# A gated cross-attention layer with a routed feed-forward: the shared first half's down products made as rounded products chunk by chunk, the scatters counted in two semaphores, and three orders changed

## The reference, cut to what matters

```python
x = x + tanh(g_xattn[0]) * xattn(layernorm(x), ctx, ctx, ...)
xf = layernorm(x)
logits = xf @ Wg                       # 16 experts, the two best are kept
gates = softmax(where(mask, logits, -inf))
for e in range(16):
    h = silu(xf @ W1[e] + b1[e]) * (xf @ W11[e] + b11[e])
    y = y + (h @ W2[e] + b2[e]) * gates[:, e, None]
z = silu(xf @ Ws1 + bs1) * (xf @ Ws11 + bs11) @ Ws2 + bs2   # the shared network
x = x + tanh(g_ffn[0]) * (y + z)
```

## Time and profile before

| | |
|---|---|
| median of 3 runs | 568.99 us |
| the profiled execution | 574.73 us |
| its span (first to last instruction) | 572.6 us |
| PE busy | 546.3 us (95%) |
| DVE busy | 353.6 us (62%) |
| POOL busy | 333.2 us (58%) |
| ACT busy | 238.5 us (42%) |

### The profile page before, as it was taken

One profiled execution on the slowest core, in us unless ns is written; L12 is line 12 of the kernel. 1 busy time (PEld: TensorE's weight loads), 2 busy tenths in 40 slices (PEclk: granted clock), 3 DMA queues, 4 the chain that ended last, 5 costly groups with the idle time before them and its releaser, 6 DMA issues.

```text
span 572.6 us, 12049 instructions
## 1 busy us (share of the span) xinstructions
PE 546.3 (95%) x3290; PEld 440.9 (77%) x3291; DVE 353.6 (62%) x861; ACT 238.5 (42%) x788; POOL 333.2 (58%) x273
## 2 busy tenths in 40 slices
PE   7889999999979999988999999999999999999996
PEld 6556667666758878777888888888888888888785
DVE  5757788787678732345665566555665556435677
ACT  1899999999994201202222122221222212232232
POOL 4689999998863486623364674444444830236550
PEclk8999999999999999999999999999999999999999
DMA  8571001000112144335458777656665210113332
GB/s 284 245 300 64 21 20 38 29 26 20 65 39 103 46 166 174 105 98 185 140 177 293 249 287 259 201 201 211 211 211 201 82 46 29 35 54 107 109 111 73
DMA packets 32899, 76.08 MB, mean 133 GB/s; under 512 B 4961, under 2 KB 21857, under 8 KB 29921
## 3 DMA queue, kind: packets, MB, share of 16 engines
q1 hardware_dynamic: 14960, 52.44, 25.5%
q10 hardware_dynamic: 14832, 14.82, 8.0%
q0 software_dynamic: 3072, 8.39, 4.7%
HBM read 54.93 MB, written 18.61 MB: 128 GB/s over the span
## 4 chain that ended last, share of the span: by engine, by line
PE 80%; DVE 8%; issue 5%; another core or an unknown queue 3%; ACT 2%; POOL 2%; DVEq 0%; ACTq 0%; POOLq 0%
PE mid L749 14%; PE big L730 8%; PE big L731 8%; PE big L732 7%; PE big L517 5%; PE big L653 4%; PE mid L740 4%; PE big L651 3%; PE big L652 3%; PE mid L530 3%; PE work L549 3%; PE last L670 2%; PE work L670 2%; PE last L542 2%
## 5 line engine op out<-in xcount | busy, mean ns | idle before, releaser
L939 ACT ACTIVATE last<-arena 128x512 f32<-128x512 f32 x47 | 28.3, 602 | 183.3 <-DVE arena L1409 183.3
L837 ACT ACTIVATE arena<-big,nmax 128x128 f32<-128x128 f32 x256 | 90.7, 404 | 9.0 <-DVE nmax L1061 8.4
L749 PE MATMUL mid<-dring,arena 128*128 x376 | 88.9, 379 | 0.0
L1409 DVE TENSOR_TENSOR arena<-big,bring 128x512 f32<-128x512 f32 x47 | 32.5, 692 | 87.2 <-PE big L732 87.2
L730 PE MATMUL big<-u_hi,xsT_hi 128*128 x188 | 81.8, 435 | 1.6 <-issue 1.6
L1572 POOL TENSOR_TENSOR u_lo<-arena,u_hi 128x2048 fp32r<-128x2048 f32 x16 | 74.4, 4652 | 1.3
L749 PEld LDWEIGHTS mid<-dring,arena 128*128 128x128 f32 x376 | 67.8, 190 | 7.4
L732 PE MATMUL big<-u_hi,xsT_lo 128*128 x188 | 73.5, 391 | 0.0
L731 PE MATMUL big<-u_lo,xsT_hi 128*128 x188 | 73.4, 390 | 0.0
L1548 POOL TENSOR_TENSOR arena<-arena,rinv 128x1024 f32<-128x1024 f32 (+1 forms) x32 | 58.7, 1834 | 13.3 <-DVE rinv L1069 13.0
L1672 POOL TENSOR_TENSOR pool_mark<-mhalf 128x1 f32<-128x1 f32 x15 | 2.9, 194 | 104.0 <-PE big L732 87.6
(11 more groups left out here) (198 smaller groups left out, 1202.9 us busy)
## 6 DMA issues: line engine op xcount, KB each, us to landing
arena<-up_w_dram SPq DMA_DIRECT2D x16, 1024.0 KB, 7.6
bring<-expert_bias_dram SPq DMA_DIRECT2D x16, 640.0 KB
dring<-down_w_dram SPq DMA_DIRECT2D x18, 512.0 KB
sorted_y<-arena ACTq DMA_DIRECT2D x47, 128.0 KB, 1.7
arena<-sorted_x ACTq DMA_DIRECT2D x43, 128.0 KB, 2.1
sorted_x<-dring SPq DMA_DIRECT2D x3, 1536.0 KB, 9.4
arena<-ctx_t_dram ACTq DMA_DIRECT2D x8, 256.0 KB, 2.8
dring<-up_w_dram SPq DMA_DIRECT2D x2, 1024.0 KB, 4.8
```

Source lines behind the costliest of these rows:

```text
L749: i = mm(mid[:, 1, 0:D], gT[:, p, c, :], dring[:, slot, c * D:(c + 1) * D], start=(c == 0), stop=(c == HC - 1))
L837: i = nc.scalar.activation(probs[:, u % 2, h, :], big[:, u % 2, h // 4, (h % 4) * CTX:(h % 4 + 1) * CTX], ACT.Exp, bias=nmax[:, u % 2, h:h ...
L1409: v.tensor_tensor(hb1[:, p, :], big[:, p, 0, :], bring[:, slot, 0:HID], ALU.add).then_inc(h1_ready, 1)
```

## The change

The first half's down products take the form that the second half's had: `shared_down` and `last_down` become one function of a chunk. The hidden chunk goes into the `gg` buffer, its two parts into `first_gs`, the two parts of the down weight into `first_d` (both laid over the part of the arena that held `gshT`). ACT makes the rounded parts, DVE the rests; the rounding of the last pair's transposed rows goes from POOL to ACT and DVE. The first two blocks' transposes go into `big`, and the remaining pieces of the shared half stand ahead of the first block's up product.

```diff
-WARM = 10
+WARM = 20
...
+        first_d = sb("first_d", [P, 2, DCOLS], F32R)
+        first_gs = sb("first_gs", [P, 2, 2, 512], F32R)
...
+        first_bank = (work, last, mid[:, 0, :], mid[:, 1, :])
+        def hidden_chunk(n):
+            return gg[:, n % 2, :] if n < HC * TILES // GROUP else gshT[:, n // HC % 2, n % HC, :]
...
 # PE, attention
-                    elif ahead:
+                    elif ahead and (behind or u == 2):
                         scores(j + 1, u - 2)
-                    if behind and u == 1:
-                        pe.wait_ge(kT_ready, DC * j + 2 * DC) if ahead else pe.wait_ge(o_taken, 2 * j - 1)
+                    if behind and ahead and u == 1:
+                        pe.wait_ge(kT_ready, DC * j + 2 * DC)
                         project_out(j - 1, 1)
...
                     transpose_probs(j, u)
+                    if not behind and u == 2:
+                        scores(j + 1, 1)
+                    if not ahead and u == 0:
+                        pe.wait_ge(o_taken, 2 * j - 1)
+                        project_out(j - 1, 1)
...
 # PE, the shared down product, now of a chunk
+            def shared_down(n):
+                h, c = divmod(n, HC)
+                pe.wait_ge(gs_lo_ready, n + 1)
+                if n == 0:
+                    pe.wait_ge(d_split, 1)
+                    pe.wait_ge(lg_taken, PAIRS)
+                    pe.wait_ge(rank_taken, 1)
...
+                for t in range(GROUP):
+                    if c == 0 and h > 0:
+                        pe.wait_ge(z_taken, GROUP * (h - 1) + t + 1)
...
+                    mm(banks[t][:, 0:D], g_hi, w_hi, start=(c == 0), stop=False)
+                    mm(banks[t][:, 0:D], g_hi, w_lo, start=False, stop=False)
+                    i = mm(banks[t][:, 0:D], g_lo, w_hi, start=False, stop=(c == HC - 1))
...
             shared_up(0, 3)
+            shared_down(0)
             pe.wait_ge(xfT_kept, 4)
...
+            for n in range(4, 8):
+                shared_up(1, n - 4)
+                shared_down(n - 3)
+            shared_down(5)
             pe.wait_ge(xfT_kept, PAIRS)
...
+            for n in range(8, 15):
+                shared_up(n // HC, n % HC)
+                shared_down(n - 2)
...
+            shared_up(3, 3)
+            shared_down(13)
+            shared_down(14)
+            transpose_rows(0, 0, big[:, 0, 0, :])
+            transpose_rows(1, 1, big[:, 0, 1, :])
+            shared_down(15)
+            pe.wait_ge(xsT_ready, 2)
+            pe.wait_ge(gsh_ready, HC * TILES // GROUP)
             up(0, 0)
-            pe.wait_ge(xsT_ready, 2)
-            shared_down(3, range(1, GROUP))
-            pe.wait_ge(z_taken, 4 * GROUP)
+            pe.wait_ge(z_taken, TILES)
...
 # PE, the end
-            for n in range(2, 4 * HC):
+            for n in range(2, 4 * HC - 2):
                 shared_up(4 + n // HC, n % HC)
-                last_down(n - 2)
-            last_down(4 * HC - 2)
-            last_down(4 * HC - 1)
+                shared_down(TILES + n - 2)
+            shared_up(7, HC - 2)
+            shared_up(7, HC - 1)
+            shared_down(TILES + 4 * HC - 4)
+            for n in range(4 * HC - 3, 4 * HC):
+                shared_down(TILES + n)
...
 # ACT
+            shared_silu(0, 0)
+            act.wait_ge(w_even, 32)
+            nc.scalar.activation(first_d[:, 0, :], dring[:, 0, :], ACT.Copy).then_inc(d_hi_done, 1)
+            round_hidden(0)
+            act.wait_ge(xfT_ready, PAIRS)
+            nc.scalar.activation(xfT_hi[:, :, 2 * P * LAST:2 * P * PAIRS], xfT[:, :, :], ACT.Copy).then_inc(xfT_hi_kept, 1)
...
+            for n in range(8, 16):
+                shared_silu(n // HC, n % HC)
+                round_hidden(n)
...
 # DVE, ahead of the places
+            keep_rest(0)
+            dve.wait_ge(d_hi_done, 1)
+            v.tensor_tensor(first_d[:, 1, :], dring[:, 0, :], first_d[:, 0, :], ALU.subtract).then_inc(d_split, 1)
             shared_hidden(0, [2])
...
+            for n in range(8, 15):
+                shared_hidden(n // HC, [n % HC])
+                if n % HC == 1:
+                    add_shared(n // HC - 1)
+                keep_rest(n)
...
 # DVE, the end: the last chunk's gated product ahead of keep_rest(14), the last two combines behind keep_rest(15)
...
 # POOL, opening: bo_g behind the first normalise, the key weight's split in two pieces at units 0 and 1
+            normalise(0, 0)
             pool.wait_ge(bo_loaded, 16)
             pool.wait_ge(tanh_ready, 1)
             g.tensor_tensor(bo_g, bo_bc, tanh_g[:, 0:1].to_broadcast([P, D]), ALU.mult).then_inc(bo_ready, 1)
-            normalise(0, 0)
-            pool.wait_ge(bo_ready, 1)
...
 # POOL, the scatters
             for t in range(TILES):
+                landed = scattered_odd if t // 2 % 2 else scattered_even
+                if t >= 4 and t % 2 == 0:
+                    pool.wait_ge(landed, 16 * TOPK * 2 * (t // 4))
                 for k in range(TOPK):
                     g.indirect_dma_start(out=sorted_x, ...
-                                         in_=xf_all[:, t, :], in_offset=None).then_inc(scattered, 16)
-                if t == GROUP - 1:
-                    keep_xfT(LAST)
-                if t % GROUP == GROUP - 1:
-                    pool.wait_ge(scattered, 16 * TOPK * (t + 1))
+                                         in_=xf_all[:, t, :], in_offset=None).then_inc(landed, 16)
```

More of the change, by code:

```diff
@@ L148, in flamingo_layer @@
         ARENA = 16128
-        arena = sb("arena", [P, ARENA])
+        with nc.sbuf_tensor("arena", [P, ARENA], F32) as whole:
+            arena = whole
+        first_d = sb("first_d", [P, 2, DCOLS], F32R)
+        first_gs = sb("first_gs", [P, 2, 2, 512], F32R)
+        sb("arena_rest", [P, ARENA - 2 * DCOLS - 4 * 512])
         taken = [0]
@@ L655, in shared_up @@
                     i.then_inc(sh_ps, 1)
[L657 to L672, removed]
+            def shared_down(n):
+                h, c = divmod(n, HC)
+                second = h >= TILES // GROUP
+                banks = last_bank if second else first_bank
+                hi, lo = rounded_chunk(n)
+                d = (d_hi, d_lo) if second else (first_d[:, 0, :], first_d[:, 1, :])
+                pe.wait_ge(gs_lo_ready, n + 1)
[3 more added lines that the diff above has]
+                    pe.wait_ge(rank_taken, 1)
+                if n == HC * TILES // GROUP:
+                    pe.wait_ge(d_split, 2)
+                    pe.wait_ge(g_ready, BLOCKS)
+                    pe.wait_ge(xsT_ready, BLOCKS)
+                    pe.wait_ge(gT_ready, BLOCKS)
+                    pe.wait_ge(y_ready, BLOCKS)
+                for t in range(GROUP):
+                    if c == 0 and h > 0:
+                        pe.wait_ge(z_taken, GROUP * (h - 1) + t + 1)
+                    g_hi, g_lo = hi[:, t * P:(t + 1) * P], lo[:, t * P:(t + 1) * P]
+                    w_hi, w_lo = d[0][:, c * D:(c + 1) * D], d[1][:, c * D:(c + 1) * D]
+                    mm(banks[t][:, 0:D], g_hi, w_hi, start=(c == 0), stop=False)
+                    mm(banks[t][:, 0:D], g_hi, w_lo, start=False, stop=False)
+                    i = mm(banks[t][:, 0:D], g_lo, w_hi, start=False, stop=(c == HC - 1))
+                    if c == HC - 1:
+                        i.then_inc(z_ps, 1)
+                    elif t == GROUP - 1:
+                        i.then_inc(gs_used, 1)
@@ L791, in _ @@
             down(BLOCKS - 1, (BLOCKS - 1) % 2)
[L793 to L811, removed]
-                    elif t == GROUP - 1:
-                        i.then_inc(gs_used, 1)
-            for n in range(2, 4 * HC):
-                shared_up(4 + n // HC, n % HC)
-                last_down(n - 2)
-            last_down(4 * HC - 2)
-            last_down(4 * HC - 1)
+            for n in range(2, 4 * HC - 2):
+                shared_up(4 + n // HC, n % HC)
+                shared_down(TILES + n - 2)
[4 more added lines that the diff above has]
+                shared_down(TILES + n)
         @block.scalar
@@ L1288, in _, with copy_rows @@
             pair(LAST, 1, False, True, False)
-            def copy_rows(b, p):
+            def copy_rows(b, p, bank=work):
                 dve.wait_ge(xs_ps, b + 1)
@@ L1437, in _ @@
             add_biases(0, 0)
-            add_shared(3, range(1, GROUP))
             copy_rows(2, 0)
@@ L1538, in bias_x @@
             def bias_x(j):
+                if isinstance(j, int) and j == 0:
+                    pool.wait_ge(bo_ready, 1)
                 pool.wait_ge(xn_ready, 2 * j + 2)
```

166 lines of the change are left out of this document (91 added, 75 removed).

## The result

The changed kernel takes **590.02 us** (median of 4, 589.06 to 592.43) where the kernel before takes 569.02 (568.74 to 569.91): ratio 1.0371, 95% interval 1.0346 to 1.0395. It is 21 us slower; 10.8 us faster was forecast. The profiled execution took 589.45 us, its span is 587.7.

What follows compares the result with a forecast made beforehand. PE, 95% busy, was taken as the bound. Opening 2.5, last pair 0.5 and shared first half 8.4 won, end 0.6 lost: 10.8 off the 568.99 us median gives 558.2 us; own range 556.3 to 561.5, with rivals 555.0 to 565.0.

Steps and rivals of the forecast that it cites:

- Scatters: POOL's scatters beside the shared first half: dropping two waits saves POOL 2.8 us; total unchanged, 6 us of room.
- DVE held by POOL: Rival, chance 0.05: from chunk 0 to the second group's end, POOL holds 14 DVE subtractions; time rises to 576 us.
- Opening and last pair: Twenty warm-ups hold PE's clock and reordered work fills waits: opening 2.5 us won, last pair 0.5 won.
- the orders: Warm-ups and instruction orders at the opening and in the first and last pairs; forecast 3.0 us won together.
- Shared first half: PE's shared downs in chunk form: 4.7 us of work and 6.5 of gaps go, 2.8 of new gaps; 8.4 won.
- End: Last up ahead of a down waits for its bank, three downs and two combines follow; 0.6 us lost.

Runs made afterwards that it cites:

- e3: Changed kernel with the old scatter waits, POOL waiting after each eighth scatter until all have landed; 565.08 us, single execution.
- e6: Changed kernel with 12 one-column products on POOL after each eighth scatter, pauses of about 2 us without any wait for landing; 568.54 us.
- e13: Changed kernel with the old scatter waits, ten warm-ups and the old instruction orders at the opening and in the first and last pairs; ratio 0.9961.
- e17: Changed kernel with old scatter waits, POOL's split of the second expert's weight behind the gates, old orders at opening and first and last pairs; 564.69 us, 0.9870.
- e9: Kernel before with only the new orders at the opening and in the first and last pairs, including twenty warm-ups; ratio 0.9992.
- e16: Changed kernel with the old scatter waits and POOL's split of the second expert's weight held until DVE has the gates; 565.58 us, ratio 0.9892.
- e5: Kernel before, unchanged, profiled once more; 571.85 us.
- e4: Kernel before with only the new scatter waits (two counts, no wait for all to have landed); 587.03 us.
- e10: Changed kernel with the old scatter waits, timed; 565.1 us, ratio 0.9922.
- e18: Changed kernel with old scatter waits, POOL's split of the second expert's weight behind the gates, and the old order at the end; 564.89 us, 0.9874.
- e14: Changed kernel with the old scatter waits and the old order at the end; ratio 0.9944.
- e12: Changed kernel with each up and down of the shared first half as one f32 product in place of three rounded ones; 596.44 us.

## Why the prediction was wrong, point by point

**Scatters: the step that failed.** It read "POOL loses two waits of 1.70 us in place of 0.30" as 2.8 us gained, and "the scatters give nothing and cost nothing, with 6 us of room". POOL's own timing came within 2.4 us (last scatter forecast at 234.7, found at 232.3), but these waits were breaks that PE needed (e3, e6). Without them the up product of chunk 9 ended 7.2 us after that of chunk 8 and chunk 10's another 22.0 later (211.63, 218.82, 240.81), where 4.18 is the pace, and chunk 11's 4.6: 3.0 + 17.8 + 0.4 = 21.2 us. No rival had it: I priced the waits on POOL and on the rows alone. The trace before held a warning, not read: its lags grow within a run of 8 scatters (0.04, 0.21, 0.42), are back at 0.04 behind the next wait, and reach 2.67 in the last run. This is the 0.42:

```profile
216.79 0.39 PE L653 MATMUL big<-xfT_hi,u_lo 128*128 128x512 f32 x1
217.60 0.69 ACT L924 ACTIVATE arena<-big,bias 128x512 f32<-128x512 f32 x1 [2.24 <-PE big L653]
```

**DVE held by POOL.** This rival was right in mechanism and wrong in place. Beside scatters the rests take 0.69 (here at 205.93); beside the split, which starts on the 16th up product just as the last two rests are due, they cost PE 4.0 us here and 4.7 in e13. I had looked for POOL's arithmetic in the scatters' stretch only. There the slow piece of the earlier trace rows lay, from 202.61 to 204.80, over POOL's rounding at 203.19 (1.05 us) more than over the subtraction at 204.32 that I named; both leave POOL with the change, so the argument stood.

```profile
205.93 0.69 DVE L1341 TENSOR_TENSOR first_gs<-arena,first_gs 128x512 fp32r<-128x512 f32 x1
```

The Trainium skill, page "SBUF — State Buffer", section "Who interferes with whom", says that the one of the two that starts second waits for the other's whole length. The trace agrees for the split (264.30 to 269.37 beside 264.19 to 268.82); scatters do not act as such an instruction here (0.69).

**Opening and last pair, 3.0.** Clock and pace came as forecast, but the warm-ups took 7.06 us in place of 6.3 and pushed the transposes back, so that the projection starts at 8.42 where it started at 8.36. The first up product starts at 174.87 in place of 176.79, but e13 and e17 have it at 174.49 and 174.55 with the old orders, and the time shows nothing of the orders (e9, and e17 against e16). The 2.49 us without work and the 3.18 us projection of the earlier trace rows are not the same in every execution: with ten warm-ups and the old orders they are 1.40 and 3.02 in e5, 0.99 and 3.25 in e4, and 1.51 and 1.92 in e17, whose projection starts at 7.38. What decides between them no run shows.

```profile
6.92 0.63 PE L472 MATMUL mid<-const,arena 128*128 128x128 f32 x4 [1.51 <-DVE arena L1059]
7.38 1.92 PE L478 MATMUL work<-arena 128*128 128x256 f32 x8
```

A term taken from one execution was mis-sized.

**Shared first half, 8.4.** Close: in e16 PE is busy all through 190 to 241 us.

```profile
190.00:220.00 30.00, 30.00 (x176) 26.56 (x175) 20.24 (x36) 9.88 (x15) 20.08 (x19) 1.00 0.42 147
220.00:241.00 21.00, 21.00 (x123) 18.52 (x122) 8.43 (x13) 5.74 (x9) 12.90 (x14) 1.00 0.29 105
```

From the first up product to the experts' second hidden transposes it takes 83.6 us there and 82.8 in e10, where it took 90.2 before and 90.0 in e5: 6.4 to 7.4 won. e17 as a whole, 7.6 us with an interval of about 5.7 to 9.2, agrees.

**End, 0.6 lost.** 0.7 lost between e16 and e18, and the other way between e10 and e14, both less than the intervals: not shown.

**Sum.** Forecast 10.8 won, measured 21.0 lost. Of the 31.8 between, 21.2 are the stall, 4.0 the held rest, 3.0 the orders. The other 3.6, in which the shared half's 1.0 to 2.0 short of 8.4 and PE's lower clock after the held rest (0.83 in 262 to 282) have a part, I did not separate.

## What to carry to other kernels

A wait that an engine makes for its own DMAs may also be a break that others live on: ahead of taking it out, look at how late the signals of the other engines arrive at either end of it. The lag between the end of a product and the start of what waits for it costs nothing while there is slack, so it shows in no total, but it can be read from the timeline in a minute. And for each DVE subtraction of two SBUF operands that is added, look which POOL arithmetic can start beside it, over the whole stretch; a collision that falls or not by the microsecond may show as spread of the times (562.3 to 569.1 in e10, 564.7 to 566.9 without it), though spread alone proves none: the kernel before has 567.8 to 572.4.

## What the runs showed of the hardware

While POOL issues indirect scatters of 128 rows every 1.27 us without a break, PE's signals arrive later and later (0.04 us, then 12.79 and 18.86), while ACT's signals to DVE (0.03) and the scatters themselves go on in time. In the changed kernel, after some 18 scatters, PE itself falls to about one instruction per 0.70 us or a multiple of it; in e4 and e12 it keeps its pace and waits for engines that wait for its signals. It hardly depends on bytes (256 or 1024 a row, 590.9 and 590.0 us) or on other loads (589.7), but on the length of the unbroken run, and perhaps on how many instructions PE issues meanwhile (e12). Breaks of 1.7 to 2.2 us after each eight prevent the stall and keep the lag under 0.8 in e3 and e6; it still reached 2.67 in the kernel before, 2.34 in e16 and 3.04 in e13, at the end of the last run. PE's granted clock fell from 1.00 to 0.50, the 1.2 GHz level, during the stall, in which PE executed 20 products in 21 us (0.56 on the mean of that stretch, 0.50 in the next), and was 0.99 from 241 us on, where PE ran without gaps again.

What it is that fills up was not settled: the signals themselves, or the records that PE leaves of its instructions. The Trainium skill, page "NOTIFIC — the notification-queue block", section "7.1 Overflow: three behaviours, one of which stalls the engine", says that the block that takes such records holds its producer back when its inner queues are full; no run here shows whether that is the path. All executions here, the timed ones too, come with a span and a granted clock from such records, so no run shows either whether the stall is there without them.
